# Last stage of a four-layer decoder: routing arithmetic spread over the recurrence, tokens in step order, expressions computed ahead

## What is computed

```python
E, D, TOP_K = (8, 128, 2)
h0 = hidden_states.mean(axis=1) @ ctx_w.T + ctx_b
xw = hidden_states @ gru_w_ih.T                    # 800 x 3072
# step(): hw = h @ gru_w_hh.T (1024 -> 3072), r, z sigmoid, n tanh
_, hs = jax.lax.scan(step, h0, jnp.swapaxes(xw, 0, 1))        # 100 steps
routing = _l2norm(jnp.swapaxes(hs, 0, 1).reshape(B, S, E, D), EPS_NORM)
expr = (hidden_states @ expr_w.T).reshape(B, S, E, D)
gram = jnp.einsum('bsed,bsfd->bsef', routing, routing)
diff_n = _l2norm(gram - jnp.eye(E), EPS_NORM)
penalty = jnp.mean(jnp.sum(diff_n ** 2, axis=(-2, -1)))       # over all tokens
num = jnp.sum(expr * routing, axis=-1)
den = max(|expr|, EPS_COS) * max(|routing|, EPS_COS)
scores = (1.0 - num / den) * (1.0 + penalty)
top_v, top_i = jax.lax.top_k(scores, TOP_K)                   # two experts a token
# out = the two experts' gated MLPs, weighted, + a shared gated MLP
```

## Time and profile before

| | us |
|---|---|
| median of 3 runs | 3506.21 (3499.66 to 3508.11) |
| the profiled execution | 3508.9 |
| its span in the trace | 3507.1 |
| PE busy in it | 3014.4 |
| DVE busy in it | 1446.5 |
| ACT busy in it | 745.8 |

### The profile page before, as it was taken

One profiled execution on the slowest core, in us unless ns is written; L12 is line 12 of the kernel. 1 busy time (PEld: TensorE's weight loads), 2 busy tenths in 40 slices (PEclk: granted clock), 3 DMA queues, 4 the chain that ended last, 5 costly groups with the idle time before them and its releaser, 6 DMA issues.

```text
span 3507.1 us, 62840 instructions
## 1 busy us (share of the span) xinstructions
PE 3014.4 (86%) x25733; PEld 1715.3 (49%) x25733; DVE 1446.5 (41%) x3572; ACT 745.8 (21%) x1844; POOL 215.3 (6%) x393
## 2 busy tenths in 40 slices
PE   6888798799888887999799769999999999983386
PEld 3554466588554444556456424444444444431185
DVE  3635254211365455102654213434343434349822
ACT  2331233211123443110133111111111111110110
POOL 3002100200200000002000000000000000000011
PEclk9989998799889999999799689999999999996698
DMA  3000000577100002210000460000000000010084
GB/s 135 1 1 1 14 6 1 188 261 273 38 1 1 1 1 86 69 48 1 1 1 1 122 183 15 12 13 12 13 12 13 12 13 12 13 47 23 25 288 158
DMA packets 75724, 185.76 MB, mean 53 GB/s; under 512 B 31120, under 2 KB 53373, under 8 KB 64158
## 3 DMA queue, kind: packets, MB, share of 16 engines
q1 hardware_dynamic: 71486, 177.17, 15.4%
q0 software_dynamic: 4096, 6.57, 0.6%
HBM read 157.79 MB, written 25.89 MB: 52 GB/s over the span
## 4 chain that ended last, share of the span: by engine, by line
PE 75%; DVE 14%; ACT 5%; issue 3%; POOL 1%; DMA 1%; another core or an unknown queue 1%; SPq 0%; POOLq 0%; DVEq 0%; ACTq 0%
PE banks L1138 29%; PE banks L969 8%; PE banks L806 4%; PE banks L529 4%; PE banks L482 3%; PE banks L700 2%; PE banks L1033 2%; PE banks L1112 2%; PE banks L1045 2%; PE banks L1171 2%; PE banks L828 2%; ACT arena L1348 2%; PE banks L846 1%; DVE peaks L1802 1%; PE banks L595 1%
## 5 line engine op out<-in xcount | busy, mean ns | idle before, releaser
L1138 PE MATMUL banks<-arena 128*32 128x384 f32 x12800 | 1032.2, 486 | 1.0 <-DVE arena L2061 1.0
L1138 PEld LDWEIGHTS banks<-arena 128*32 128x32 f32 x12800 | 431.9, 110 | 601.6 <-issue 599.6
L2073 DVE TENSOR_TENSOR arena<-banks,arena 128x256 f32<-128x256 f32 x200 | 84.9, 425 | 448.3 <-PE banks L1138 448.3
L1481 ACT ACTIVATE arena<-arena 128x256 f32<-128x256 f32 x200 | 83.3, 416 | 753.7 <-DVE arena L2073 753.7
L1224 ACT ACTIVATE arena<-banks 128x512 f32<-128x512 f32 (+3 forms) x129 | 73.2, 574 | 528.8 <-PE banks L1033 151.2
L969 PE MATMUL banks<-arena 128*128 128x400 f32 x512 | 172.5, 499 | 1.5 <-DVE arena L2023 0.8
L806 PE MATMUL banks<-arena 128*100 128x256 f32 x512 | 147.6, 445 | 18.2 <-ACT arena L1406 5.4
L529 PE MATMUL banks<-XNT,arena 128*128 128x400 f32 x384 | 150.8, 535 | 9.0 <-ACT XNT L1235 3.7
L700 PEld LDWEIGHTS banks<-arena 32*121 32x121 f32 x1536 | 105.6, 196 | 62.0 <-ACT arena L1326 46.9
L969 PEld LDWEIGHTS banks<-arena 128*128 128x128 f32 x512 | 97.1, 190 | 76.8 <-DVE arena L2023 1.4
L1686 DVE TENSOR_REDUCE arena<-banks 100x4 f32<-100x1444 f32 x64 | 106.3, 1661 | 61.1 <-PE banks L656 60.8
(11 more groups left out here) (318 smaller groups left out, 4060.4 us busy)
## 6 DMA issues: line engine op xcount, KB each, us to landing
arena<-fc SPq DMA_DIRECT2D x22, 1024.0 KB, 6.3
arena<-pj SPq DMA_DIRECT2D x22, 1024.0 KB, 5.2
arena<-gu SPq DMA_DIRECT2D x21, 1024.0 KB, 7.0
arena<-whh SPq DMA_DIRECT2D x32, 384.0 KB, 36.6
arena<-dn SPq DMA_DIRECT2D x21, 512.0 KB, 4.9
arena<-xw SPq DMA_DIRECT2D x400, 24.0 KB
xw<-arena SPq DMA_DIRECT2D x6, 1536.0 KB, 5.2
arena<-hh SPq DMA_DIRECT2D x16, 512.0 KB, 3.3
```

The lines of the kernel that those rows point to most:

```text
L1138: last = nc.tensor.matmul(banks[32 * j:32 * j + 32, 2 * c + i, 0:384].rearrange("p (g n) -> p g n", g=3), hT[:, 1 - i, 32 * ub:32 * ub + 3 ...
L1481: nc.scalar.activation(rz[:, c, :], pre[:, c, :], ACT.Sigmoid).then_inc(sem["rz_done"], 1)
L2073: nc.vector.tensor_tensor(pre[:, c, :].rearrange("p (g n) -> p g n", g=2), banks[:, 2 * c + i, 0:2 * P].rearrange("p (g n) -> p g n", g=2) ...
```

## The change

- **Tokens in step order.** `XNT` of this stage, `xw` and `history` now hold token (s, b) at place s*8+b. `xw` has 16 more rows so that the last two steps can load ahead as well.
- **Expressions made ahead.** `ew` is loaded into buffers that the recurrence uses later. PE makes all expressions, 14 further units, right behind the input products, and SP stores them to `shown`.
- **Weight loads between stores.** Of the 32 `whh` loads 8 are issued first, then 4 behind each of the first six stores of `xw`.
- **Dots lap by lap.** The 100 steps are 10 laps of 10. In laps 1 to 9, DVE does behind each step one of the ten products and its reduction for the 80 tokens of the lap before. SP loads `seen` (the lap's states) and `expr` (320 KB each) once a lap. The last lap's ten stand behind the recurrence. The copies of the lower triangle are made once for all laps. DVE's and SP's loops now hold 10 steps; PE's and ACT's still two.
- **Scores.** The small arithmetic runs on 80 partitions x 10 laps; the scores go through DRAM (`score_rows`, one store, one load) to get back to 100 positions x 8 sequences.
- **End.** DVE runs `shared_rows` ahead of `pairs_back`. `down` takes every eighth column of `h3`.

```diff
+LAP = 10
+LAPS = S // LAP
+ROWS = LAP * B
-            for b in range(B):
-                for j in range(2):
-                    tokens("a", [(XNT[:, kk, b * S:(b + 1) * S], ew[:, kk, 512 * j:512 * j + 512]) for kk in range(C)], 512)
 ...
+            pe.wait_ge(sem["l_ew"], 16)
+            for i in range(TILES):
+                token_products(i, ew, 2)
 ...
+            def dots_of(k, chunk):
+                into = prod[:, k % 2, :]
+                if k < 3:
+                    x, y = ((expr, expr), (expr, seen), (seen, seen))[k]
+                    last = nc.vector.tensor_tensor(into, x, y, ALU.mult)
 ...
+                else:
+                    s_ = k - 2
+                    m = E - s_
+                    step(nc.vector.tensor_tensor(into[:, 0:m * ED], seen[:, 0:m * ED], seen[:, s_ * ED:], ALU.mult))
+                    dst = gram[:, chunk, s_:s_ + (m - 1) * (E + 1) + 1:E + 1]
+                last = nc.vector.tensor_reduce(dst, into[:, 0:m * ED].rearrange("p (o e d) -> p o e d", o=1, d=ED), AX, ALU.add)
 ...
+            with dve.Fori(1, LAPS) as lap:
+                for k in range(LAP):
+                    step_of(k % 2, lambda a, b_: (a * LAP // 2) * lap + (a * (k // 2) + b_))
+                    if k == 0:
+                        dve.wait_ge(sem["l_expr"], 16 * lap)
+                    if k == 1:
+                        dve.wait_ge(sem["l_seen"], 16 * lap)
+                    dots_of(k, bass.ds(lap - 1, 1))
+                settled()
 ...
-            for b in range(B):
-                gb = gram[:, b, :].rearrange("p (e f) -> p e f", e=E)
-                step(nc.vector.tensor_tensor(gb, gb, t(3)[:, b, :].unsqueeze(2).to_broadcast([S, E, E]), ALU.mult))
-                step(nc.vector.tensor_tensor(gb, gb, t(3)[:, b, :].unsqueeze(1).to_broadcast([S, E, E]), ALU.mult))
+            g4 = gram.rearrange("p c (e f) -> p c e f", e=E)
+            step(nc.vector.tensor_tensor(g4, g4, t(3).unsqueeze(3).to_broadcast([ROWS, LAPS, E, E]), ALU.mult))
+            step(nc.vector.tensor_tensor(g4, g4, t(3).unsqueeze(2).to_broadcast([ROWS, LAPS, E, E]), ALU.mult))
 ...
-            step(nc.vector.tensor_copy(t(1), t(0)))
+            dve.wait_ge(sem["l_score"], 32)
+            step(nc.vector.tensor_copy(small[:, 1], small[:, 0]))
 ...
-            pairs_back(1)
-            shared_rows(lambda b: phase_over() if b % 4 == 3 else None)
+            shared_rows()
+            pairs_back(1, lambda g: phase_over() if g % 2 else None)
 ...
+            sp.wait_ge(sem["scored"], 1)
+            sp.dma_start(score_rows.rearrange("(c p) e -> p c e", p=ROWS), tabs[:, 0]).then_inc(sem["l_score"], 16)
+            sp.wait_ge(sem["l_score"], 16)
+            sp.dma_start(small[:, 0], score_rows.rearrange("(s b) e -> s b e", b=B)).then_inc(sem["l_score"], 16)
```

More of the change, by code:

```diff
@@ L1464, in _ @@
             stream("C")
[L1466 to L1471, removed]
+            for b in range(B):
+                evac(XNT[:, :, b:T:B], P, 2 * S)
+            for i in range(2 * TILES):
+                rows = min(P, T - i % TILES * P)
+                if i >= 2:
+                    act.wait_ge(sem["xw%d" % (i % 2)], 16 * (i // 2))
+                for q in (0, 2, 4) if i < TILES else (0,):
                     evac(xw_out[0:rows, i % 2, 512 * q:512 * q + 512], rows, 512)
-            n.add("d_evac", 1 + 3 * TILES)
+            n.add("d_evac", 1 + 4 * TILES)
             nc.scalar.preload_act_table(ACT.Sigmoid)
@@ L1484, in _ @@
                         nc.scalar.activation(cand[:, us], t1[:, us], ACT.Tanh).then_inc(sem["n_done"], 1)
-            for b in range(B):
[L1486 to L1490, removed]
+            for i, norms in enumerate((dots[:, 0:2], tabs[:, 7])):
                 act.wait_ge(sem["root_in"], i + 1)
@@ new lines, in _ @@
+            dve.wait_ge(sem["l_expr"], 16 * LAPS)
+            dve.wait_ge(sem["l_seen"], 16 * LAPS)
+            for k in range(LAP):
+                dots_of(k, slice(LAPS - 1, LAPS))
+            sort_tables()
+            dve.wait_ge(sem["seen_used"], LAPS + 1)
+            for s_ in range(1, E):
+                m = E - s_
+                last = nc.vector.tensor_copy(gram[:, :, E * s_:E * s_ + (m - 1) * (E + 1) + 1:E + 1],
+                                             gram[:, :, s_:s_ + (m - 1) * (E + 1) + 1:E + 1])
@@ L2113, in _ @@
+            step(last)
+            t = lambda i: tabs[:, i]
             step(nc.vector.tensor_copy(gram[:, :, 0:E * E:E + 1], dots[:, 0]))
@@ new lines, in _ @@
+            with sp.Fori(0, LAP // 2) as t:
+                for i in range(2):
+                    transfers_of(2 * t + i, i, lambda a, b_: a * t + b_)
+            with sp.Fori(1, LAPS) as lap:
+                for i in range(2):
+                    sp.wait_ge(sem["l_h%d" % i], 64 * LAP // 2 * lap + 64)
+                sp.wait_ge(sem["seen_used"], lap)
+                sp.dma_start(seen, seen_rows[bass.ds(lap - 1, 1)].rearrange("o p g -> (o p) g")).then_inc(sem["l_seen"], 16)
+                for k in range(LAP):
+                    transfers_of(LAP * lap + k, k % 2, lambda a, b_: (a * LAP // 2) * lap + (a * (k // 2) + b_))
+                    if k == LAP // 2:
+                        sp.wait_ge(sem["expr_used"], lap)
+                        sp.dma_start(expr, expr_rows[bass.ds(lap, 1)].rearrange("o p g -> (o p) g")).then_inc(sem["l_expr"], 16)
```

277 lines of the change are left out of this document (144 added, 133 removed).

## The result

The changed kernel took 3351.48 us (median of 4 runs, 3348.68 to 3355.40), the kernel before 3502.93 us beside it (4 runs, 3499.59 to 3508.11). The ratio is 0.9567, with a 95% interval of 0.9549 to 0.9585. The forecast was 3355, between 3343 and 3382. The profiled execution of after spans 3353.6 us, that of before 3507.1.

A forecast was written before the change was run, and what follows sets the result against it. PE alone bounds the recurrence, DVE the dots behind it; at the very end everything waits. Terms -5.7 - 133.05 - 0.7 + 2.4 - 14.4 = -151.5 us took 3508.9 to 3357.4, so 3355 against the median; range 3343 to 3382.

The forecast's parts named there:

- Room in the recurrence: Recurrence: one product and reduction behind each step fits DVE's idle time, so the moved work costs 0.
- the margin of 4.36 us: Recurrence step: DVE's 3.52 us idle plus 0.84 us slack of the turned state; only longer dots delay a step.
- Preparation: Before the recurrence: 14 added units cost 24.5 us, 28.4 idle and 1.8 go; -5.7 us, range -7 to +3.
- The rival of the preparation as DMA bound: Before the recurrence: slower stores make PE slip 8 us, total 3363; chance 0.10.
- Dots: Behind the recurrence: seven of eight batches go (-133.7 us); with copies, tables and start, -133.05 us.
- the remaining group: Behind the recurrence: the last lap's batch stays, one of eight at 19.1 us, less 1.2 for its copies.
- Scores: Score arithmetic behind the dots: fewer scalings -1.9 us, wider operations +0.9, small ones +0.3; -0.7 us.
- the way through DRAM: Scores' store in 800 pieces of 32 B and one load, taken as 5.0 us, half of it hidden.
- Pair count: PE's count after the scores: starts after 9.5 us instead of 7.1, so +2.4 us, range 0 to +5.
- End: Kernel's end: shared expert's additions go ahead of the gathered rows; -14.4 us, range 0 to -14.4.
- The cover that the prediction named: Kernel's end: PE and DVE otherwise free from 3461 to 3486, about 25 us, hiding doubled strided weight loads.
- The rival of the lap's end: Recurrence: DVE stalls fetching instructions at lap branches; one fetch, 3.0 us, hidden, two, 6.0, cost 21 us: 3376; chance 0.12.

The follow-up runs named there:

- no_dots: The changed kernel without the dot products and reductions in laps 1 to 9, their loads and waits kept: 3353.5 us, ratio 0.9557.
- weights_first: The changed kernel with all 32 recurrent weight loads issued ahead of the first store, as before: 3378.74 us, ratio 0.9602.
- tail_alone: The kernel before with only the new order of the last two parts: 3490.23 us, ratio 0.9958.
- long_body: The changed kernel with 60 small memsets in each of five steps, DVE's loop body growing from 248 to 548 instructions: 3369.47 us, ratio 0.9582.

## Why the prediction was right

The total, 3355 against 3351.5, came out by its own steps: no step is off by more than 3 us. That the sum is so close is in part luck. The profiles differ by 153.5 us where 151.5 were forecast; the dots gave 2.8 more than forecast, preparation and scores 1.5 more, and the pair count took 2.1 of it back.

- **Room in the recurrence.** Right. 0 forecast, 0 measured; `no_dots` shows that the dots cost nothing, and the doubled and tripled pairs that the margin of 4.36 us was read correctly, from the turning's row and not from DVE's busy share.
- **Preparation.** -5.7 forecast, -6.5 measured. That the 28.4 us idle came from the order of SP's queue is shown by `weights_first` (+30.5). The rival of the preparation as DMA bound did come about in a small way, at the store of the seventh tile (9.3 us), and the banks absorbed it; DMA was busy 0.88 of that stage.
- **Dots.** -133.05 forecast with their start, -135.8 measured (-134.9 and -0.9). The term that was mis-sized is the remaining group. It was taken as an eighth of the batches of before, 19.1 less 1.2 = 17.9; it took 16.4, its tables 0.6 instead of 1.35, its seven copies 0.8 instead of 1.6. The price per operation was right, 1.22 us at 1024 columns on 80 partitions as on 100. What the forecast carried over are the waits between them: before, each operation starts some 0.03 us after the one ahead has ended; now a product starts up to 0.08 us before the reduction ahead of it ends.
- **Scores.** -0.7 forecast, -1.4 measured, the way through DRAM 2.0 + 1.6 us and 3.9 with its gaps, where 5.0 were taken. Up to the count +2.1, forecast +2.4. From PE's last recurrence product to the penalty product it was 39.5 us; the prediction wrote 41, though its own terms give 43 (177 less 133.05 and 0.7).
- **Pair count.** The step that failed. "Instead of 7.1 the count starts after 9.5" was right, and priced the wait at its own length only; it left out what 2.2 us of idleness do to the granted clock behind it. That cost another 2.1 us.
- **End.** -14.4 forecast, -14.3 in the trace, -14.2 by `tail_alone`. The cover that the prediction named for the strided loads was not even needed.
- **The rival of the lap's end** was rightly put beside the forecast and rightly kept small. Its reason for being small, that a fetch would be 3.0 us and hidden, was not what saved the kernel: nothing is fetched at the branches. The 1.1 us of its sum were read from a queue whose packets hold 16 KB each; those of DVE's queue hold 8. Where the body is fetched again, a stall is 3.7 to 4.4 us, between the 3.0 and the 6.0 of the prediction. PE lost 14.2 us by it in `long_body`, whose memsets had used up part of the room; behind the last pair alone, 0.7 us, a stall of 3.7 would make 4.4 us and so just fill the margin (an estimate from these rows).

## What to carry to other kernels

When an engine sets the pace of a long loop, read from one iteration how late its partner may be, the idle time plus the slack of the result that is needed first, and put arithmetic from behind the loop there up to that sum; doubling the moved work is a cheap test of the number. A larger body is free only while the instruction queue of that engine shows no packets at the loop's branches back. A queue that carries large loads and small stores deserves its order as much as its volume, and a wait on PE is worth its length plus the slower clock of what comes next.

## What the runs showed of the hardware

- A DVE loop of 248 or 268 instructions was fetched in its first lap (4 packets) and then no more; one of 288 fetched 39 packets in 900 us and stalled 4.4 us at each branch back, one of 548 fetched 59 and stalled 3.7 us.
- After an idle time of 1.84 to 4.90 us, small products of PE took up to 1.9 times as long, 2.68 us instead of 1.43 for sixteen, at granted clocks of 0.50 to 0.63; after 1.43 us only the second half of them was slower; after 0.60 us or none they ran at 1.00.
- Weights read with a stride of eight words have records of 262 ns a load instead of 167, and the stream of products over them the same 14.0 us.
- The 800 pieces of 32 B of the score rows landed in 2.0 us and came back in 1.6 us.
